# Leaving out the GpSimd drain that closes a fused depool and mixture-of-experts kernel on Trainium2

## What is computed

```
x = x + xattn(layernorm(x), ctx, patch_lens)
    # h      = rmsnorm(embeds, g_res) @ W_in.T + b_in
    # patch  = rmsnorm(ctx, g_init)[..., :256]
    # depool = a scan over the patches with constant decay, gathered by the
    #          cumulative count of patch boundaries, and added to h
x = x + ffn(layernorm(x))
    # probs  = softmax(x @ gate_w); the two best of E = 8 experts, weights renormed
    # out    = sum over a row's two experts of
    #          weight * ((silu(x @ w1[e]) * (x @ w3[e])) @ w2[e])      (F = 1024)
```

## Time and profile before

| what | value |
|---|---|
| median of 3 runs | 471.37 us (471.29 to 472.96) |
| device time of the profiled execution | 469.25 us |
| span of the profiled execution | 467.7 us |
| of that, granted TensorE clock, mean | 0.925 |
| TensorE (PE) matmuls busy | 398.7 us, 85% |
| VectorE (DVE) busy | 314.1 us, 67% |
| ScalarE (ACT) busy | 193.3 us, 41% |
| GpSimd (POOL) busy | 203.5 us, 44% |

### The profile page before, as it was taken

The page is one execution under the profiler, slowest core; times in us unless marked ns, Lnnn a source line. Parts: engine busy times, 40 slices in busy tenths (PEclk is TensorE's granted clock), DMA queues, the critical chain, the costliest instruction groups (busy, mean ns, idle before and its releaser), DMA issues.

```text
span 467.7 us, 11843 instructions
## 1 busy us (share of the span) xinstructions
PE 398.7 (85%) x2269; PEld 343.0 (73%) x2270; DVE 314.1 (67%) x835; ACT 193.3 (41%) x334; POOL 203.5 (44%) x215
## 2 busy tenths in 40 slices
PE   0768895427899999999999999999999999799770
PEld 0657784415678888888888888888888888688660
DVE  7986876899785578537767765776776557475420
ACT  2455445202443545335635533553553345353320
POOL 5355544222343467335645553664654324223311
PEclk9979787556999999999999999999999999899986
DMA  6947785701787688657887986797797555445521
GB/s 186 333 170 237 254 261 172 257 2 34 236 245 221 167 251 250 191 163 206 242 254 201 272 247 158 222 287 209 223 260 220 149 164 140 122 112 146 157 46 11
DMA packets 79130, 89.79 MB, mean 192 GB/s; under 512 B 6871, under 2 KB 59351, under 8 KB 79111
## 3 DMA queue, kind: packets, MB, share of 16 engines
q1 hardware_dynamic: 64279, 55.23, 36.5%
q0 software_dynamic: 14832, 34.35, 29.2%
HBM read 58.76 MB, written 30.80 MB: 192 GB/s over the span
## 4 chain that ended last, share of the span: by engine, by line
PE 70%; DVE 7%; issue 4%; DMA 2%; POOL 1%; ACT 1%; DVEq 1%; ACTq 0%; POOLq 0%
PE bank L1439 66%; PE bank L1446 2%; DMA dg<-depool_rows,plugi 1%; DVE ctx_sb L978 1%; DMA out<-yblk,itok 1%; POOL dg L481 1%; ACT split L342 1%; PE bank L1372 1%; PE bank L1393 1%; DVE split L348 1%; DVE split L1229 0%; DVE batch L1066 0%; PE bank L1318 0%; DVE onehot_lo L1062 0%; POOL out L521 0%
## 5 line engine op out<-in xcount | busy, mean ns | idle before, releaser
L1439 PE MATMUL bank<-split,xT_hi 128*128 x592 | 170.7, 411 | 7.0 <-DVE split L348 3.3
L1439 PEld LDWEIGHTS bank<-split,xT_hi 128*128 128x128 f32 x592 | 108.1, 191 | 30.5 <-issue 8.9
L1439 PEld LDWEIGHTS bank<-split,hT 128*128 128x128 f32 x888 | 112.3, 193 | 4.9 <-issue 1.0
L1439 PE MATMUL bank<-split,hT 128*128 (+1 forms) x888 | 113.6, 284 | 1.3 <-ACT yblk L684 0.7
L521 POOL DMA_INDIRECT out<-yblk,itok x37 | 76.5, 2067 | 74.1 <-ACT yblk L684 65.6
L677 ACT ACTIVATE gact<-bank 128x512 f32<-128x512 f32 x74 | 44.2, 598 | 145.7 <-PE bank L1439 145.7
L1177 DVE TENSOR_TENSOR hmul<-gact,bank 128x512 f32<-128x512 f32 x74 | 50.8, 687 | 75.9 <-ACT gact L677 75.6
L1439 PE MATMUL bank<-split,xT_lo 128*128 x296 | 94.1, 399 | 0.0
L513 POOL DMA_INDIRECT xblk<-z_rows,gidx x40 | 41.2, 1030 | 88.9 <-DVE gidx L1216 80.9
L348 DVE TENSOR_TENSOR split<-raw,split x22 | 50.4, 2293 | 28.4 <-ACT split L342 28.4
L1439 PEld LDWEIGHTS bank<-split,xT_lo 128*128 128x128 f32 x296 | 56.8, 192 | 13.7
(11 more groups left out here) (196 smaller groups left out, 335.3 us busy)
## 6 DMA issues: line engine op xcount, KB each, us to landing
raw<-in_L_ffn_w POOLq DMA_DIRECT2D x84, 256.0 KB
swap_rows<-swap_in SPq DMA_DIRECT2D x74, 256.0 KB, 3.1
swap_out<-swap_rows SPq DMA_DIRECT2D x74, 256.0 KB, 3.2
ctx_sb<-in_ctx SPq DMA_DIRECT2D x4, 1024.0 KB, 6.4
raw<-in_L_ffn_w SPq DMA_DIRECT2D x12, 256.0 KB, 4.7
x_all<-in_x SPq DMA_DIRECT2D x4, 512.0 KB, 8.2
depool_rows<-gact SPq DMA_DIRECT2D x4, 512.0 KB, 3.1
out<-x_all SPq DMA_DIRECT2D x4, 512.0 KB, 4.6
```

The source lines that it names most:

```text
L1439: mm = pe.matmul(out_, xp, w_, start=start and n == 0, stop=stop and n == 2)
```

## The change

The block is opened with the option that leaves out GpSimd's drain at its end. Nothing else in the source is touched:

```
@@ -267,7 +267,7 @@
         parked = [[sem(f"parked{q}_{part}") for part in range(2)] for q in range(2)]
         swapped = [[sem(f"swapped{q}_{part}") for part in range(2)] for q in range(2)]
 
-        block = stack.enter_context(nc.Block())
+        block = stack.enter_context(nc.Block(no_gpsimd_drain=True))
 
         def pair(t, n):
 
```

## The result

The changed kernel takes 464.51 us (463.8 to 465.89, 4 runs), the one before 471.33 us (470.81 to 472.96, 4 runs with one more than shown above). The ratio is 0.9866, with a 95% interval of 0.9834 to 0.9898: 1.3% faster, which is 6.3 us of 471.33 (4.8 to 7.8); the two medians themselves lie 6.8 us apart. The profiled execution took 464.25 us, with a span of 462.6 us.

What follows compares the result with a forecast made beforehand. TensorE, busy 85% of 467.7 us, bounds the kernel, but GpSimd's closing drain alone sets its end. Removing 6.4 us, with nothing added or moved, takes the 471.37 us median to 465.0 us; range 462.8 to 468.2 us.

Steps and rivals of the forecast that it cites:

- The path at the end: End of program: GpSimd's 6.363 us drain alone sets the end, after all transfers have landed.
- the sum: Whole kernel: 6.4 us removed at the block's end, nothing added or moved; span 467.7 to 461.3 us.
- Added at nothing: Block's end: one more semaphore instruction on each of four other engines, costed at nothing under 6.0 us of GpSimd cover.
- Every wait in the steps stays: Steps before the block's end: instructions unchanged, so DMA queues, clock and waits stay; nothing moved.
- The price of a transfer: GpSimd's closing drain: 6363 ns divided evenly over 180 issued transfers, estimated at 35 ns each.
- the turning point: Later cost of 180 leftover entries: above 49 ns each, the change would turn out slower.
- the slower rival: After the program or in the next execution: 180 leftover entries worked off dearer, 483 us at 100 ns each; chance 0.04.
- The drain moves behind the program: Beyond the span: the drain's work is done there, time outside grows 1.6 to 8.0 us, total stays 471.4; chance 0.08.
- The half-way form: Beyond the span: about half of the drain's time comes back, giving 468.2 us; chance 0.03.
- The bookkeeping is paid dearer later: Close of execution or next one's first GpSimd transfers: 180 entries worked off one by one, 483 us; chance 0.04.
- second sign: Start of program: GpSimd's first transfers, 633 ns each at L467, would be slower than before.
- A miss of the waits: Block's end: the 6.4 us is a transfer landing the closing waits miss, so time stays 471.4 us; chance 0.01.

Runs made afterwards that it cites:

- the ladder: Kernel before plus, behind its closing waits, a drain, then groups of 1 to 180 extra transfers, each waited for and drained; drains 0.047 us plus 82 ns per transfer up to 96.

## Why the prediction was right

- **The path at the end.** That GpSimd's drain stood alone there, with nothing moving or computing, was read from the stretch table and the L70 view, and holds: with the drain back alone the time is back too (ratio 1.0005), and the tail went from 10.98 to 4.59 us, 6.39 against the 6.4 of the sum.
- **Added at nothing.** ScalarE's extra semaphore instruction came 6.2 us before it could matter; the cover was put at 6.0 us.
- **The size.** 465.0 us was forecast from 471.37 - 6.4, and 464.51 measured. Against the before median of the same set, 471.33 - 6.4 = 464.9 us; the rest is within the runs' spread of about 2 us.
- **The profiled span** was put at 461.3 us and came out at 462.6. "Every wait in the steps stays" failed for this execution: its last addition was issued 1.4 us later, most of it because the clock was at 1.2 GHz for longer ahead of the end. The medians don't show such a shift; that they were free of it is in part luck, since single runs of one kernel lie some 2 us apart.
- **The price of a transfer.** "6363 / 180 = 35 ns for each" was the weakest step, and wrong: the price is 82 ns, for 77 of them. The division was even over all, and the runs say that most were no longer on record. The forecast didn't rest on it, but the turning point of the slower rival did: it asked what 180 entries would cost later, and 77 were left. Its price per entry should have been (6.4 + 2.4) / 77 = 114 ns, above what a drain needs, so that the rival was further off than it was told.
- **Slips that change nothing.** 461.0 - 456.67 is 4.3 us, not 4.4; in the changed kernel it was 462.4 - 458.06 = 4.3 us. The 466.8 us called the lower bound of the gain isn't worked out anywhere. And the chain of waits does follow sequencers (it has steps such as "POOLq L335"); it misses the drain because it starts from the last instruction that isn't a sequencer's.
- **The drain moves behind the program.** Out: the time beyond the span is 1.6 us before and after. By the Trainium skill's "VectorE: DVE Perf Modes", section "The DRAIN you can't avoid", short drains stand on all engines behind the program. No trace here shows one; if one does stand on GpSimd, it didn't take the work over. The half-way form is out too: 468.2 us is a ratio of 0.9934, above the interval.
- **The bookkeeping is paid dearer later.** Out as a slower time. Its second sign, a slower start, is absent as well: GpSimd's first transfers take a median of 582 ns (583 before), and its drain at the start 169 ns as before, not the 6.4 us that 77 entries would cost. Whether an execution of this kernel came directly ahead of the profiled one isn't on record. What becomes of the 77 entries isn't seen in these traces, nor what a different program started next would find. The two source views of the changed kernel:

```profile
L1527 POOLq DRAIN  x1: 169/169/169, 0.5 to 0.5; - x1
L467 POOL DMA_DIRECT2D out<-zeros x3: 518/582/795, 15.2 to 16.5; - x3
```

- **A miss of the waits.** Out as well: the closing waits end 0.2 us before the span does.

## What to carry to other kernels

Look at what stands between the last landing and the end of the span. The chain of waits doesn't show it, since it starts from the last instruction that isn't a sequencer's; a source view of the line that the block is opened in does. In this kernel each transfer of GpSimd was waited for by a semaphore, and its closing drain only tidied up, at a price that went with the transfers still on record. In such a kernel it can be left out, or, where it is to stay, moved to a stretch in which GpSimd waits anyway; that gained as much here, within the runs' spread, though its last 0.5 us weren't hidden. It only pays where GpSimd comes last, and not every transfer counts: what has been retired on the way is free by then.

## What was not expected of the hardware

- GpSimd's drain cost 0.047 us and 82 ns for each transfer on record, the same for 16 and for 128 rows, and came out alike to the nanosecond in four kernels (6363 ns). The count on record is known in the ladder's short groups; for this kernel (77) it is worked out from the price.
- In the ladder, GpSimd halted for 2.96 us after 128 transfers of 16 rows and for 3.24 us after 113 of 128 rows, and the drain behind had only the later ones to pay for. If the halt is the retiring, it is at most 23 ns for each in the first case, less than a third of what a drain takes for one; the last of the 128 was itself still landing in the first 1.2 us or so of it (1.7 us from issue to landing, of which its issue took 0.48).
- A drain's work ran beside a transfer in flight, and its record in the profile counts the time for which the engine is still busy ahead of it (1.49 of 7.86 us).
